# Linear attention in a four-layer metaformer: another order of the groups' steps on TensorE, ScalarE and VectorE, and the end of the layer norm on GpSimd

## What is computed

```python
x_ext = concat([x.reshape(b, c, n), memory], axis=2)
q, k, v = split(einsum('oc,bcn->bon', W_qkv, x_ext), 3, axis=1)
q = softmax(to_heads(q), axis=2) * SCALE        # over the 16 channels of a head
k = softmax(to_heads(k), axis=3)                # over the positions
context = einsum('bhdn,bhen->bhde', k, v)
out = einsum('bhde,bhdn->bhen', context, q)[..., :n]
y = einsum('oc,bcn->bon', W_out, out) + b_out
y = (y - mean(y)) / sqrt(var(y) + 1e-5) * ln_g + ln_b   # over the channels
x_residual = x_residual + y
```

## Time and profile before

| what | us |
|---|---|
| median of three runs | 1105.27 (1104.97 to 1107.36) |
| span of the profiled execution, first to last instruction | 1104.3 |
| first keys of the stage on TensorE | starts at 27.69 |
| last instruction of the stage, VectorE L729 | ends at 116.99 |
| first instruction of the next stage, VectorE L1653 | starts at 117.54 |
| busy in the stage's window 55.20 to 82.80 (27.60 us): PE, VectorE, ScalarE, GpSimd | 21.99, 21.54, 13.99, 3.82 |

### The profile page before, as it was taken

How to read it: one execution, slowest core, us unless ns; L and a number is a source line. 1 busy time by engine, 2 the same in 40 slices (tenths; PEclk the granted TensorE clock), 3 DMA queues, 4 the chain that set the end, 5 groups by cost and what they waited for, 6 DMA issues and landing times. The chain is left out here.

```text
span 1104.3 us, 21444 instructions
## 1 busy us (share of the span) xinstructions
PE 864.2 (78%) x6822; PEld 579.7 (52%) x6822; DVE 735.0 (67%) x1964; ACT 629.9 (57%) x1293; POOL 285.6 (26%) x313
## 2 busy tenths in 40 slices
PE   4877134999999916678888867996877999958597
PEld 2665112999999915556666643443443444425232
DVE  7677788664444446878888877887585445445775
ACT  5553300654444435588888845885655777746353
POOL 3012302777777714400000002112130010025100
PEclk9889555999999966579999987997797999989699
DMA  4000271330000020101111100000100000000000
GB/s 129 1 0 0 51 132 31 93 88 20 23 22 25 19 91 1 39 30 58 38 57 38 48 20 1 1 1 21 38 1 1 1 0 0 1 12 10 1 1 38
DMA packets 25270, 32.66 MB, mean 30 GB/s; under 512 B 11582, under 2 KB 14665, under 8 KB 24814
## 3 DMA queue, kind: packets, MB, share of 16 engines
q1 hardware_dynamic: 20206, 27.50, 8.8%
q0 software_dynamic: 4992, 4.22, 1.5%
HBM read 19.31 MB, written 4.91 MB: 22 GB/s over the span
## 5 line engine op out<-in xcount | busy, mean ns | idle before, releaser
L1798 DVE SCALAR_TENSOR_TENSOR routed_hid_stage<-ps,routed_act_stage 128x512 f32<-128x512 f32 (+1 forms) x117 | 70.6, 604 | 100.1 <-ACT routed_act_stage L1566 98.7
L1566 ACT ACTIVATE routed_act_stage<-ps 128x512 f32<-128x512 f32 x117 | 69.9, 598 | 87.2 <-PE ps L1871 86.0
L1881 PE MATMUL ps<-w_sb,routed_hid_stage 128*128 x936 | 117.6, 269 | 0.0
L1128 ACT ACTIVATE hid_stage<-ps,b_col_sb 128x512 f32<-128x512 f32 x192 | 116.0, 698 | 0.0
L1871 PE MATMUL ps<-routed_x_stage,w_sb 128*128 128x256 f16 x858 | 114.9, 276 | 0.8 <-ACT routed_x_stage L1574 0.8
L1881 PEld LDWEIGHTS ps<-w_sb,routed_hid_stage 128*128 128x128 f32 x936 | 113.6, 192 | 1.5
L412 POOL TENSOR_TENSOR st_sb<-st_sb,neg_half_sb 128x4 f32 (+1 forms) x32 | 37.5, 1173 | 252.8 <-DVE st_sb L407 252.8
L1622 POOL DMA_INDIRECT routed_got_stage<-expert_rows,take_stage x78 | 81.6, 1047 | 78.1 <-DVE give_stage L1773 54.6
L1079 PE MATMUL ps<-x_sb,w_sb 128*128 (+1 forms) x384 | 94.5, 388 | 2.8 <-ACT hid_stage L1128 2.8
L1093 PE MATMUL ps<-hid_stage,w_sb 128*64 128x512 f32 x384 | 93.5, 606 | 1.3 <-DVE gated_stage L1160 1.3
L1871 PEld LDWEIGHTS ps<-routed_x_stage,w_sb 128*128 x858 | 84.3, 104 | 9.4 <-issue 1.1
(11 more groups left out here) (404 smaller groups left out, 1861.9 us busy)
## 6 DMA issues: line engine op xcount, KB each, us to landing
w_stage_sb<-f_w SPq DMA_DIRECT2D x32, 176.0 KB
x_sb<-w_sb SPq DMA_DIRECT2D x16, 256.0 KB, 2.4
rt_sb<-vals_stage SPq DMA_DIRECT2D x16, 256.0 KB, 2.3
rel_bias_sb<-bias_bands SPq DMA_DIRECT2D x16, 128.0 KB
w_stage_sb<-f_w SPq DMA_DIRECT2D x14, 128.0 KB, 3.0
w_sb<-f_w SPq DMA_DIRECT2D x1, 1536.0 KB
routed_got_stage<-expert_rows,take_stage POOLq DMA_INDIRECT x78, 2.5
expert_out<-routed_rows_stage,give_stage POOLq DMA_INDIRECT x78, 2.2
```

What stands on the lines that cost most here:

```text
L1128: nc.scalar.activation(hid[:, n % RING, :], ps[:, n % BATCH, :], func, bias=b1_col[:, b:b + 1], scale=UNSCALE).then_inc(h_act, 1)
L1566: nc.scalar.activation(act_h[:, n, :], ps[:, H1 + (q + n) % 2, :], ACT.Silu, scale=UNSCALE).then_inc(h_act, 1)
L1798: last = nc.vector.scalar_tensor_tensor(hid[:, q % 2, n, 0:full], ps[:, H3 + (q + n) % 2, 0:full], UNSCALE, act_h[:, n, 0:full], ALU.mult, ...
L1881: last = nc.tensor.matmul(ps[:, Y + q % 2, h * C:(h + 1) * C], hid[:, q % 2, n, a * BLK + h * P:a * BLK + (h + 1) * P], w2[:, bass.ds(e * ...
```

## The change

Only `linear_attention()` changes, and what it computes stays the same.

- GpSimd takes the end of the layer norm: `finish` is now there, and uses a new tile `y_fin`. After the power it issues three operations on 128 x 256 elements: `y` times the inverse deviation (the latter repeated along the channels), times `ln_g`, and the sum into `x_tok`. The addition of `ln_b` stands ahead of them. A new semaphore `y_taken` tells VectorE that `y_tok` may be overwritten; `centre` waits for it. GpSimd's operations follow each other by semaphore waits on itself.
- VectorE loses L724 and L729. The mask stands ahead of `query_sums`, the scaling of the mix ahead of `query_ready`.
- TensorE computes keys and queries two groups ahead, behind the mix of `g`; turns the keys of `g + 1` in front of the mix of `g`; turns the queries of `g + 1` at the end of the iteration of `g`. The 4 spare matmuls before the mix are gone.
- `x_grp` and its 8 copies on ScalarE are gone; the matmuls read `x16`. `square` stands behind the values.
- All loops over groups are written out. VectorE's subtraction of the query maxima waits until TensorE has turned the queries of the group before.

```diff
@@ scalar
-                        if squared is not None:
-                            square(squared)
                         act.wait_ge(values_ps, g + 1)
                         nc.scalar.activation(v_tok[:, :, :], v_ps, ACT.Copy, scale=UNSCALE).then_inc(v_copied, 1)
-                        if not last_group:
-                            nc.scalar.copy(x_grp[:, :], x16[:, bass.ds((g + 1) * GTOK, GTOK)]).then_inc(x_copied, 1)
...
+                    for g in range(GROUPS + 1):
+                        if g + 1 < GROUPS:
+                            exps(g + 1)
+                            take_values(g + 1)
+                        if g >= 1:
+                            square(g - 1)
+                        if g + 1 < GROUPS:
+                            take_turned(g + 1)
+                            take_queries(g + 1)
@@ tensor
+                    for g in range(GROUPS):
+                        context(g)
+                        if g + 1 < GROUPS:
+                            project(1, g + 1).then_inc(values_ps, 1)
+                            turn_keys(g + 1)
+                        mixed(g)
+                        if g + 2 < GROUPS:
+                            keys(g + 2)
+                            pe.wait_ge(q_shifted, g + 2)
+                            project(0, g + 2).then_inc(queries_ps, 1)
+                        if g + 1 < GROUPS:
+                            spare(5, 2)
+                        out(g)
+                        if g + 1 < GROUPS:
+                            spare(5, 2)
+                            turn_queries(g + 1)
@@ gpsimd
+                    def finish(g):
+                        xg = x_tok[:, g * TPG:(g + 1) * TPG, :]
+                        c.link(nc.gpsimd.tensor_tensor(xg, xg, rows(2), ALU.add))
                         pool.wait_ge(y_var, g + 1)
                         nc.gpsimd.tensor_tensor(y_st[:, 3, :], y_st[:, 2, :],
                                                 neg_half[:, :].broadcast_to((P, TPG)), ALU.pow).then_inc(y_rstd, 1)
+                        pool.wait_ge(y_rstd, g + 1)
+                        nc.gpsimd.tensor_tensor(y_fin[:, :, :], y_tok[:, 0, :, :],
+                                                y_st[:, 3, :].unsqueeze(2).broadcast_to((P, TPG, C)),
+                                                ALU.mult).then_inc(y_taken, 1)
+                        pool.wait_ge(y_taken, g + 2)
+                        c.link(nc.gpsimd.tensor_tensor(y_fin[:, :, :], y_fin[:, :, :], rows(1), ALU.mult))
+                        c.link(nc.gpsimd.tensor_tensor(xg, xg, y_fin[:, :, :], ALU.add))
@@ vector
                         dve.wait_ge(y_ps, g + 1)
+                        dve.wait_ge(y_taken, g + 1)
...
-                    def finish(g):
-
-                        dve.wait_ge(y_rstd, g + 1)
-                        for t in range(TPG):
-                            last = nc.vector.scalar_tensor_tensor(y[:, t, :], y[:, t, :], y_st[:, 3, t:t + 1],
-                                                                  ln_rows[:, 1, :], ALU.mult, ALU.mult)
-                        c.link(last)
-                        dve.wait_ge(x_biased, g + 1)
-                        xg = x_tok[:, bass.ds(g * TPG, TPG), :]
-                        c.link(nc.vector.tensor_tensor(xg, xg, y, ALU.add))
...
+                        if g >= 1:
+                            dve.wait_ge(qt_ps, g)
...
+                        masked(g)
+                        if g + 1 < GROUPS:
+                            query_sums(g + 1)
+                        scaled(g)
+                        if g + 1 < GROUPS:
+                            query_ready(g + 1)
+                        if g >= 1:
+                            variance(g - 1)
```

More of the change, by code:

```diff
@@ L635, in group, with context @@
                         last.then_inc(qt_ps, 1)
[L636 to L638 removed]
+                    def context(g):
                         pe.wait_ge(v_copied, g + 1)
@@ L655, in group, with out @@
                         last.then_inc(mix_ps, 1)
-                        if not last_group:
-                            turn_keys(g + 1)
-                        spare(5, 2)
+                    def out(g):
                         pe.wait_ge(mix_ready, g + 1)
@@ L756, in key_inverse, with masked @@
                         c.link(nc.vector.reciprocal(k_inv[:, :], k_inv[:, :]))
-                    def group(g, first=False, last_group=False):
-                        if not last_group:
-                            maxima(g + 1)
-                        if not first:
-                            centre(g - 1)
-                        if not last_group:
-                            query_sums(g + 1)
+                    def masked(g):
                         dve.wait_ge(ctx_ps, g + 1)
@@ L788, in _ @@
                     key_inverse(0)
-                    group(0, first=True)
-                    with dve.Fori(1, GROUPS - 1) as g:
-                        c.loop(g, 11, start=1)
-                        group(g)
-                    c.end(GROUPS - 2)
-                    group(GROUPS - 1, last_group=True)
-                    for part in (centre, variance, finish):
-                        part(GROUPS - 1)
+                    for g in range(GROUPS):
+                        if g + 1 < GROUPS:
+                            maxima(g + 1)
+                        if g >= 1:
+                            centre(g - 1)
+                        masked(g)
+                        if g + 1 < GROUPS:
+                            query_sums(g + 1)
+                        scaled(g)
+                        if g + 1 < GROUPS:
+                            query_ready(g + 1)
+                        if g >= 1:
+                            variance(g - 1)
+                        if g + 1 < GROUPS:
+                            dve.wait_ge(mix_ready, g + 1)
+                            key_inverse(g + 1)
+                    centre(GROUPS - 1)
+                    variance(GROUPS - 1)
         router_ps, exp_in, exp_done = (sem(f"moe_{n}") for n in ("router_ps", "exp_in", "exp_done"))
```

74 lines of the change are left out of this document (31 added, 43 removed).

## The result

The changed kernel takes 1087.27 us (median of four runs, 1086.62 to 1088.35) against 1105.25 us before in the same series: ratio 0.9841, 95% interval 0.9825 to 0.9857, 18.0 us less. The profiled execution has a span of 1086.4 us and a time of 1088.35 us, 1.1 us above the median. In every run of this case that lists both, the time lies 1.7 to 2.5 us above the span; by that the profiled execution before, with its span of 1104.3 us, took some 1106 us (an estimate), about as far above its median, so the two spans can be compared.

What follows compares the result with a forecast made beforehand. VectorE was taken as the bound, TensorE barely under it. Start -4.1, middle -16.3 and end +1.3 us gave -19.1 us, so 1105.27 would become 1086.2 us, range 1081.5 to 1092.

Steps and rivals of the forecast that it cites:

- The bound and the steps: Middle groups: VectorE sets the pace, TensorE needs 6.64 us, barely under it, GpSimd 4.54 us; waits for keys and queries go.
- VectorE's turn: VectorE's chained work in one middle group after the change: 6.85 us if nothing holds it up.
- The hold: VectorE's L711 waits for GpSimd's sum on the shared SBUF port: 0.30 us a group, making 7.15 us.
- the middle: Five middle groups at 7.15 instead of 10.41 us each: 16.3 us less.
- signs named for being right: Mixes 7.0 to 7.3 us apart, TensorE over 90% busy at clock 1.00, L711's successor 0.6 to 0.8 us, among others.
- the rival without a hold: No hold, first context at full clock: 6.85 us a group, 22.8 us less in all, 1082.5 us; chance 12%.
- TensorE: TensorE's work in a middle group at full clock: 6.64 us, so it will look nearly full.
- The slower rival: TensorE at its lower clock becomes the bound, 13.3 us a group, 1123 us; chance 2%.
- The start: Start of the stage: mix 1 at 44.4 instead of 48.55 us, 4.1 us less.
- The end: From mix 6 to the stage's end: 17.7 instead of 16.41 us, through waits for the first product and holds, 1.3 us more.
- Nothing lost later: Behind the stage: none of the gain is lost, the next stage starting 0.55 us after the last instruction.

Runs made afterwards that it cites:

- e12: Changed kernel with two y_tok/y_st sets, offsets added at the start, last group finished on VectorE, no four spares, and the keys' inverse sums on GpSimd: 1081.17 us.
- e1: Changed kernel with the layer norm's end (scalings and sum into the residual) back on VectorE, new order kept: 1098.45 us, ratio 0.9947.
- e2: Changed kernel with TensorE, ScalarE and VectorE back in the old order, layer norm's end still on GpSimd: 1099.09 us, ratio 0.9949.
- e7: Changed kernel with keys and queries computed one group ahead instead of two, turns still ahead of the mix: 1091.87 us, ratio 0.9872.
- e3: Changed kernel with one more GpSimd operation per group, 128 x 512 elements, result unread, ahead of the sum into the residual: 1086.35 us, ratio 0.9850.
- e8: Changed kernel with two sets of y_tok and y_st, ln_b added for all groups at the start, last group finished on VectorE: 1084.54 us, ratio 0.9823.
- e10: The changed kernel itself, unaltered, run again in a second series: 1087.02 us, ratio 0.9851.
- e4: Changed kernel without its last four spare matmuls a group: 1082.87 us, ratio 0.9802, in the first series.

## Why the prediction held, and where it was off

**The bound and the steps**: right in the main. VectorE's list sets the pace once the layer norm's end has left and the waits for keys and queries are gone; GpSimd has room in its own work, but the loop through it and the lock, which the prediction did not walk as a loop, is just as long (e12); TensorE is nearly full at 1.00. e1, e2 and e7 take away a part each, and the predicted waits come back.

**VectorE's turn**, 6.85 us: measured 6.92. The difference is the round trip from the mask to the scaling, with 0.23 us of wait for the mix in it: 1.24 us (58.31 to 59.55) instead of the 1.17 taken from rows 5.

**The hold**, 0.30 us: this is the term that was off. It measured 0.00 in the middle groups, so a group takes 6.92 instead of 7.15 us, and the middle gave 17.5 us instead of 16.3. Two of the signs named for being right did not come, mixes 7.0 to 7.3 us apart and the successor of L711 at 0.6 to 0.8 us; the middle came as the rival without a hold said. I had L711 arrive at 3.52 us behind L717 and GpSimd done at 3.82. It arrived at 3.51 (54.46 to 57.97), but GpSimd was done at 3.65: the product with the repeated deviation took 0.61, not 0.73 us, and hand-overs 0.07 to 0.09, not 0.12, while the power began 0.32, not 0.25 us behind L753. The last 0.14 us of overlap cost nothing: a held `centre` ends 0.27 to 0.29 us behind GpSimd, and one of 0.43 us that starts 0.14 us early ends there anyway. The 128 x 2 operation of 0.16 us in e2 ended 0.02 us behind. In both, about 0.14 us of the operation's own length is missing behind the release, as if its start could run beside GpSimd (an estimate from these rows). In e7, with 0.19 us of overlap (59.05 to 59.24), `centre` took 0.47 us. That the lock is there was right: 0.84 and 0.87 us in the tail, 0.72 in e3, 0.80 in e12, and the held 128 x 2 operations of e2 and e8. The Trainium skill (SBUF — State Buffer, section "SBUF: two separate sides") has the engine that comes first keep the shared port pair for its whole instruction while the other is blocked. These rows agree in kind; by the rule alone the overlap of 0.14 us would have been a short hold too, and the rows show none.

**TensorE**, 6.64 us of work at 1.00: in the changed kernel 45.22 of 46.00 us busy, and without the spares 41.89. The slower rival did not come. In the middle groups of e1 the clock fell, behind TensorE's gap (0.31 us of work in 50 to 52 us).

**The start**: mix 1 at 44.95 us, 3.6 instead of 4.1 us earlier. It varies with the clock at the head of the stage. The window from 34 to 36 us in the changed kernel:

```profile
34.00:36.00 2.00, 2.00 (x15) 1.88 (x12) 1.84 (x4) 0.53 (x2) 0.00 (x0) 0.61 0.03 8
```

The same window in e10, the same kernel again:

```profile
34.00:36.00 2.00, 2.00 (x14) 1.67 (x14) 1.90 (x5) 1.36 (x6) 0.00 (x0) 1.00 0.03 8
```

And in e8:

```profile
34.00:36.00 2.00, 2.00 (x11) 1.24 (x9) 1.82 (x5) 1.36 (x4) 0.28 (x1) 0.50 0.00 0
```

With 0.61, 1.00 and 0.50 granted there, mix 0 stands at 38.41, 37.46 and 40.43 us. e8 has its hold of L775 ahead of that; e4, the same as the changed kernel up to mix 0, was granted 0.50 there and has its mix 0 at 39.67 us.

**The end**: 17.1 us behind mix 6 instead of the predicted 17.7, through the predicted waits for the first product (1.71 and 1.96 us) and the holds. e8 shows that they were on the path, with 2.2 us.

**Nothing lost later**: wrong for this execution, though e10 does not show it as a cost of the change. In the stage the sum came to -3.6 - 17.5 + 0.7 = -20.4 us, 1.3 more than predicted; 0.35 us went at the meeting of the engines (0.90 instead of 0.55 us) and 2.1 us behind it. From the next stage's first instruction to the end of the span it was 986.8 us before (1104.3 - 117.54), 988.9 after, 985.0 for the same kernel in e10, and 981.0 (e7) to 988.9 over all fourteen profiled executions. A part shows in the routed experts, where ScalarE's L1605 waited 3.8 us for landings, against 2.1 us before (L1581) and 2.2 us in e10. So 1.3 us too much in the stage and 2.5 us behind it partly cancelled, and that 1086.2 met 1087.27 to 1.1 us is in part luck.

## What to carry to other kernels

Where an engine's turn holds a wait and a block of work that another engine could do, take both away together: here each alone gave two fifths of the gain or less (4.5 and 5.6 of 20.0 us at the next stage, 6.0 and 6.7 of 18.0 in time, 1.41 and 0.50 of 3.49 a group), because the next wait stood right behind. Before shortening the engine that seems to set the pace, walk every loop through the engines, shared ports included; a second loop of the same length (here variance, GpSimd, lock, `centre`) eats the gain. Work moved to GpSimd also has to be placed so that it does not run beside VectorE's operations on two SBUF operands: e2 lost 0.43 us a group where it did, and e8 had a hold of 0.53 us once. In a long program, read a change by distances inside its stage, and repeat the unaltered kernel in the same series before trusting 4 us of the whole.

## What the runs showed of the hardware

- `centre`'s VectorE operation on 128 x 256 elements with two SBUF operands, when it met a GpSimd operation, ended 0.27 to 0.29 us behind it (0.72 us in e3, 0.80 in e12, 0.84 and 0.87 in the changed kernel's tail, instead of 0.43). Begun 0.14 us ahead of that end, it was not lengthened; begun 0.19 us ahead (e7), it took 0.47 us. A 128 x 2 operation of 0.16 us was held as well (0.59 us in e2, 0.69 in e8) and in e2 ended 0.02 us behind. The GpSimd operation of 128 x 256 behind such a `centre` took 0.79 to 0.80 instead of 0.72 us.
- On GpSimd, 128 x 256 elements took 0.72 to 0.74 us, and 0.61 us with a second operand repeated along the channels; 128 x 512 elements with both operands the same repeated tile took 1.04 us (e3); the power took 1.02 us for 128 x 4 and 0.71 us for 128 x 2 (e12).
